# Moving the third depthwise unit of a step ahead of projection, transposes and mix in a windowed channel-attention kernel

## The reference

```python
qkv = einsum('bchw,oc->bohw', gn(x), w_qkv) + b_qkv        # 64 -> 192 channels
qkv = depthwise_conv3x3(qkv, w_dw, padding=1) + b_dw
q, k, v = windows of 8 x 8 pixels, 4 heads of 16 channels   # 1024 windows in all
attn = softmax(einsum('nhcx,nhdx->nhcd', q, k) * temperature)  # channels x channels, 16 x 16 per head
out = einsum('nhcd,nhdx->nhcx', attn, v)
gate = gelu(einsum('nhcx,yx->nhcy', v, w_mlp) + b_mlp)
y = x + einsum('bchw,oc->bohw', windows back to image(out * gate), w_proj) + b_proj
```

## Time and profile before

| | |
|---|---|
| median of 3 runs | 827.38 us (827.29 to 830.31) |
| profiled execution | 824.44 us |
| its span, first to last instruction | 822.7 us |
| mean granted TensorE clock | 0.992 of full speed |
| PE, PEld busy | 718.9 us (87%), 620.3 us (75%) |
| DVE, ACT busy | 615.0 us (75%), 506.1 us (62%) |
| DMA | 73.13 MB, 89 GB/s over the span |

### The profile page before, as it was taken

How to read it: one execution, slowest core, us unless ns; L and a number is a source line. 1 busy time by engine, 2 the same in 40 slices (tenths; PEclk the granted TensorE clock), 3 DMA queues, 4 the chain that set the end, 5 groups by cost and what they waited for, 6 DMA issues and landing times.

```text
span 822.7 us, 29929 instructions
## 1 busy us (share of the span) xinstructions
PE 718.9 (87%) x13704; PEld 620.3 (75%) x13704; DVE 615.0 (75%) x1021; ACT 506.1 (62%) x628; POOL 0.3 (0%) x5
## 2 busy tenths in 40 slices
PE   3968898989988898999989898999989898989965
PEld 3956777777877777887868787887878777877854
DVE  2715497989897886878777886868777787868676
ACT  2553465767566565767576575766566665758554
POOL 0000000000000000000000000000000000000000
PEclk9999999999999999999999999999999999999997
DMA  9723131533334040405023040403022140412022
GB/s 235 266 102 110 18 110 54 177 88 131 112 100 141 5 159 3 158 3 171 5 67 111 17 162 4 161 3 139 25 73 92 40 123 2 159 18 104 3 65 40
DMA packets 26461, 73.13 MB, mean 89 GB/s; under 512 B 9464, under 2 KB 15992, under 8 KB 21272
## 3 DMA queue, kind: packets, MB, share of 16 engines
q1 hardware_dynamic: 26076, 69.31, 26.6%
q10 hardware_dynamic: 258, 1.90, 1.2%
HBM read 54.43 MB, written 16.78 MB: 87 GB/s over the span
## 4 chain that ended last, share of the span: by engine, by line
PE 77%; DVE 11%; issue 5%; ACT 5%; DMA 1%; DVEq 0%; ACTq 0%
PE work L600 24%; PE work L580 18%; PE turn_ps L666 8%; PE gate_ps L645 8%; PE score_ps L679 7%; PE work L551 5%; DVE z L343 4%; PE turn_ps L654 4%; PE score_ps L636 3%; ACT v_t L297 2%; ACT z L275 2%; DMA z<-in_hot 1%; DVE scores L462 1%; DVE total L458 1%; ACT scores L291 1%
## 5 line engine op out<-in xcount | busy, mean ns | idle before, releaser
L580 PE MATMUL work<-consts,patches 64*100 64x192 f32 x2048 | 203.8, 337 | 14.3 <-DVE patches L407 6.5
L600 PE MATMUL work<-z,dw 109*64 109x64 f32 x6144 | 199.6, 223 | 13.2 <-DVE z L343 12.3
L600 PEld LDWEIGHTS work<-z,dw 109*64 109x64 f32 x6144 | 187.3, 138 | 22.0 <-issue 14.6
L580 PEld LDWEIGHTS work<-consts,patches 64*100 64x100 f32 x2048 | 156.0, 164 | 39.3 <-issue 11.4
L275 ACT ACTIVATE z<-work 100x768 f32<-100x768 f32 x158 | 121.5, 809 | 86.1 <-PE work L580 86.1
L275 ACT ACTIVATE qkv<-work 128x1024 f32<-128x1024 f32 x63 | 64.5, 1024 | 128.4 <-PE work L600 128.4
L343 DVE COPY z<-work 100x768 f32<-100x768 f32 x98 | 91.2, 954 | 33.4 <-PE work L580 32.6
L666 PE MATMUL turn_ps<-v_t,probs_t 64*64 64x64 f32 x2048 | 74.2, 222 | 30.9 <-ACT v_t L297 20.6
L666 PEld LDWEIGHTS turn_ps<-v_t,probs_t 64*64 64x64 f32 x2048 | 65.5, 136 | 46.3 <-ACT v_t L297 29.4
L645 PE MATMUL gate_ps<-consts,qkv 128*128 128x128 f32 x512 | 74.6, 289 | 24.7 <-issue 23.3
L343 DVE COPY qkv<-work 128x1024 f32<-128x1024 f32 x33 | 40.4, 1225 | 73.3 <-PE work L600 73.3
(11 more groups left out here) (45 smaller groups left out, 640.2 us busy)
## 6 DMA issues: line engine op xcount, KB each, us to landing
staged<-in_x SPq DMA_DIRECT2D x18, 1024.0 KB, 5.0
out_y<-staged SPq DMA_DIRECT2D x15, 1024.0 KB, 5.2
T<-in_x SPq DMA_DIRECT2D x12, 1152.0 KB, 8.8
seen<-in_x SPq DMA_DIRECT2D x16, 512.0 KB, 3.8
qkv<-in_x SPq DMA_DIRECT2D x6, 1024.0 KB, 24.9
T<-in_x SPq DMA_DIRECT2D x3, 1088.0 KB, 9.3
z<-in_edges SPq DMA_DIRECT2D x5, 288.0 KB
out_y<-staged SPq DMA_DIRECT2D x4, 256.0 KB, 3.8
```

The source lines that it names most:

```text
L580: last = nc.tensor.matmul(to[0:NPATCH, t, b * QKV:(b + 1) * QKV], patches[image, b, g], w1[image], start=True, stop=True)
L600: last = nc.tensor.matmul(to[h * HW:(h + 1) * HW, m // 8, m % 8 * NW:(m % 8 + 1) * NW], dw[0:K, c, :], z[0:K, c, :], start=True, stop=True)
```

## The change

In a third or fourth step (`a >= 2`) PE issues all three depthwise units ahead of `project(i - 1)`, `turn_v(i)` and `apply_probs(i)`; so far the third came behind `apply_probs(i)`. The variance unit, which follows v2 in step 26, stays behind `apply_probs`. DVE copies the third unit directly behind its transpose of the probabilities, ahead of the residual, the statistics and `normalise`; so far it came behind them.

```diff
@@ DVE, in the loop over steps
                 gate_up(i)
                 divide(i)
                 turn(i)
+                if n < CHUNKS and a >= 2:
+                    evacuate_dw(dve, copy, n, 3 * a - 4)
                 if i:
                     residual(i - 1)
                 if i < 2 * BANDS:
...
                 if n < CHUNKS and a < 2:
                     for g in range(8 * a + 5, 8 * a + 8):
                         evacuate_mix(dve, copy, n, g)
-                if n < CHUNKS and a >= 2:
-                    evacuate_dw(dve, copy, n, 3 * a - 4)
             mix(STEPS - 1)
             residual(STEPS - 1)
@@ PE, in the loop over steps
                 units_now = fillers(i)
-                cut = (2, 4, 6) if i % BATCHES < 2 else (1, 2, 2)
+                cut = (2, 4, 6) if i % BATCHES < 2 else (1, 3, 3)
```

## The result

The changed kernel takes 800.47 us (median of 4 executions, 799.05 to 801.96) against 827.34 before (median of 4): ratio 0.9679, interval 0.9656 to 0.9703. Its profiled execution took 801.96 with a span of 800.2, against 824.44 and 822.7, so the two profiles differ by 22.5 us. Two things are to be explained: 2.5 us between the forecast and the profiles, and 4.4 between profiles and medians.

The account below looks back on a forecast made before the run. PE, busy 87%, was taken as the bound, with 23.3 us of gaps before the gates. Ten boundaries gave 15.1, those with statistics 3.6, between pairs 1.3: 20.0 us off 827.38, forecast 807.4, range 804 to 815.

Parts of the forecast that it names:

- the price of the gap: Steady chunk boundary: PE's wait ahead of the gates goes, from v4 to gates 7.52 us instead of 9.03, gain 1.51.
- v3's copy: Fourth step: v5 needs the PSUM buffer that ACT's copy of v3 frees; spare 1.9 us, so no cost.
- the 0.3 spares of DVE and ACT: Steady boundary: DVE's scores copy and ACT's work before the first channel unit's copy each fit with 0.3 us spare.
- B: Rival: DVE becomes the bound at every boundary, its scores copy late; 15 gains of 0.6, 818 us; chance 0.12.
- C: Rival: something other than v5's copy holds the gates back, so the gap stays, 827.4 us; chance 0.05.
- D: Rival: the two PSUM buffers bind, v2 and v5 wait for ACT, slower, about 846 us; chance 0.03.
- Third step: 0, bounded by 0.07 a step either way.: Third step: v2's 2.0 us simply changes places, gain 0; bound for changed transitions 1 us over 15 chunks.
- v5 again 2.02: Fourth step on PE: v5 directly behind v4 was taken to add 2.02 us, v4's own spacing to the projection.
- With statistics: Boundaries after steps 3, 7, 11: DVE also runs statistics, gain 0.85 us each; after step 15, 1.0.
- PE's waits on patches: After steps 3, 7, 11, 15, PE was expected to wait some 0.3 us for patches (line 407).
- Between the image pairs: Gap of 3.16 us: 0.8 gained since normalise waits for ACT's square root, plus 0.46 for v2's copy; together 1.3.
- I take the same gain there.: Median of runs, 827.38, lies 2.94 us above the profiled 824.44; the same gain of 20.0 gives 807.4.

Follow-up runs that it names:

- the run without the loads: Changed kernel with the second pair's statistics taken from the two pieces loaded first, the other 14 loads left out, against the kernel before: ratio 0.9644.
- either half alone: Kernel before with only PE's new order, DVE's copies as before: ratio 1.0256; with only DVE's new order, PE as before: ratio 1.0898.
- PE's half alone: Kernel before with PE's new order only, DVE copying the third unit last as before: ratio 1.0256.
- the fill: Kernel before with additional matmuls on constants into the gate buffer at each chunk boundary: ratio 1.0016 with 8 matmuls, 0.9985 with 4.

## Why the prediction was right or wrong

Right were the bound (the copy of v5 ahead of the gates), the direction, the price of the gap (1.51 of the steady 1.94) and what hides the rest: v3's copy was there in time, the 0.3 spares of DVE and ACT were 0.19 and 0.33, and DVE bounds the boundaries with statistics. Rivals B, C and D fell: no wait on patches at steady boundaries, no gap left, no wait of depthwise units on ACT. The Trainium skill, *Perfetto Trace Analysis* (Optimization Strategy), says that a repeated bubble can mean too little SBUF or PSUM for the next tile. It was not so here: the 15 gaps, 23.3 us, went by the order of work alone, with the two buffers as they were.

Wrong was the size. The steps that failed:

1. **"Third step: 0, bounded by 0.07 a step either way."** It is 0.31 in each of 15 chunks, 4.7 us. The working took the old spacing of each piece (2.02 and 1.08) as that piece's own length. A spacing belongs to a pair of neighbours: a second depthwise unit in a row adds 1.86 (3.88 less 2.02), and scores behind the mix start before it has ended. The spacing of two like neighbours stood in the trace of before, where all six units of the first chunk run in a row, and was not used. They take 11.42 us; the last is 2.09 long, so each of the five ahead of it adds (11.42 - 2.09) / 5 = 1.87:

```profile
80.26 11.42 PE L600 MATMUL work<-z,dw 109*64 109x64 f32 x384 [1.26 <-DVE z L343]
```

2. **Fourth step, "v5 again 2.02".** The same, 0.15 in each of 15 chunks: 2.2 us.
3. **With statistics.** 0.85 was forecast for each of the first three boundaries and 1.0 for the fourth. The three chunks from the second gates on (139.72 to 279.16 before, 139.53 to 277.50 after) became 1.47 shorter in all, 0.49 each. PE's waits on patches are as forecast (0.23 to 0.30). With 0.85 (1.0 at the last) and the 0.46 of the transitions it would have been 3.9 to 4.1. The missing 2.4 to 2.6 are "issue" gaps, to which the prediction gave no term: 0.84, 0.97 and 1.18 amid depthwise units in these three chunks (and 0.50 in the one ahead of them), where the kernel before has one of 0.61 ahead of a projection (and one of 0.41 behind them). The 0.85 itself was right: in the run without the loads, where these gaps are gone, such a chunk is 44.72 long (184.62 to 229.34), and one of the kernel before without such a gap 46.05 (139.72 to 185.77), which is 1.33 more, 0.85 and 0.46 all but 0.02.
4. **Between the image pairs.** 0.8 and 0.46 were forecast. The 0.46 came. The wait of 2.36 on patches was followed by a granted clock of 1.2 GHz, which cost about 1.35 us: the chunk is 47.41 long, where 43.70 and 2.36 make 46.06. In the second profile of this kernel the same wait (2.37) is followed by the full clock, and the chunk is 46.13 long. The first profile's windows:

```profile
411.00:413.70 2.70, 0.38 (x28) 0.24 (x18) 2.63 (x5) 2.40 (x4) 0.00 (x0) 0.92 0.00 0
413.70:416.50 2.80, 2.75 (x18) 2.61 (x20) 2.73 (x6) 0.81 (x1) 0.00 (x0) 0.50 0.00 0
```

In sum: 20.0, and 6.9 from points 1 and 2, less about 2.5 for point 3 and 1.4 for point 4, is 23.0; the profiles differ by 22.5. The other 0.5 fits the 0.03 between gates and scores, 15 times. Start and end of the kernel cancel: the first gates come 1.0 later (94.09 against 93.09; 93.39 in the second profile), and what follows the last gates at a boundary is 1.0 shorter. That 20.0 came as near to 22.5 as it did is luck in part, since 6.9 too little and some 4 too much stand against each other.

5. **"I take the same gain there."** The profiled execution of the kernel before (824.44) was taken as 2.94 below the median by an offset that the change would keep. No such offset is fixed: the changed kernel's profile lies 1.5 above its median, and that makes the 4.4 us between 22.5 and 26.9. Over 68 executions of the kernel before, time and mean granted clock go together (correlation -0.89, 0.6 us for each 0.001): 0.995 goes with 824.4 on average, 0.991 with 827.1, 0.987 with 829.1. Their mean is 0.9898, and the profile, with 0.992, has no drop ahead of its last 25 us: by the slope, 1.3 of its 2.9 us. The changed kernel's profile doesn't follow the slope: with 0.993 against a mean of 0.9918 over 10 executions it should lie 0.7 below the median and lies 1.5 above, though it has the drop of 1.35 between the image pairs. So by the mean clock 0.6 of the 4.4 us are explained, and the rest is scatter of single executions whose source stays open. The second profiles of both kernels have spans of 823.1 and 798.4, 24.7 apart and not 22.5. Of the gain of the medians, the mean clock, 0.0020 higher, makes 1.2 us by the slope. Whether it is the boundary gaps that cost it in the kernel before was tried by filling them, and not settled.

The range was too narrow on the fast side: its lower end, 804, was the sum of all gaps, as if nothing but gaps could be gained and one profile fixed the level.

## What to carry to other kernels

Where an engine waits for another at a boundary, see which piece it did last, and put work that nobody waits for behind the piece that all wait for; then put the copy of that piece first on the other engine too, since either half alone cost 2.6% and 9% here. Where pieces are reordered on TensorE, take their cost from pairs of neighbours as they will stand, not from their old spacing, and let the range go beyond the gaps that can be removed. Make the sum against several executions with their granted clocks, as one profile can lie at an end of the scatter.

## What the runs showed of the hardware

- Two depthwise units in a row take 3.88 us, one alone between other pieces 2.02; mix and scores in a row take 1.55, each next to another piece 1.08 and 0.63.
- A gap of the same 1.78 us is followed by the full clock at one boundary and by 1.2 GHz at another, in one execution (PE's half alone), which costs 1.36 us; 68 executions of one and the same kernel lie 9.5 us apart (823.9 to 833.5) with mean clocks of 0.995 to 0.982.
- Gaps of 0.5 to 1.2 us in the middle of PE's units, with no releaser in the profile, come up to 5 us behind stretches of busy transfers. In the changed kernel those are pieces of 0.5 and 1.1 MB issued back to back (DMA engines busy for 0.86 of 4 us), and the gaps go but for one of 0.32 when the smaller ones are left out and T's load moves forward by 8 us. Behind other transfers shorter ones stand too: one of 0.51 where the fill has 4 matmuls (DMA 0.93 of 4 us, no statistics under way). The row of that gap and the window ahead of it, with the columns as above:

```profile
349.04 0.68 PE L600 MATMUL work<-z,dw 109*64 109x64 f32 x15 [0.51 <-issue]
340.00:344.00 4.00, 4.00 (x62) 3.16 (x60) 3.77 (x7) 3.51 (x5) 0.00 (x0) 1.00 0.93 342
```
